# Masks taken off the matrix engine: block mask by GpSimd in batch rows 1 to 3, triangles of narrow score squares added in a shared bank by VectorE

## The reference

```python
xn = _layernorm(x, axis=-1)
x = x + _L0_attn_ref(xn, ...) + _L0_ffn_ref(xn, ...)

# attention: 16 heads of 16, 4 batches of 1024 tokens, width 256
q, k = (rope(q), rope(k))
att = jnp.einsum('bhqd,bhkd->bhqk', q, k) / scale
mask = jnp.tril(jnp.ones((t, t), dtype=bool))
att = jnp.where(mask, att, -jnp.inf)
att = jax.nn.softmax(att, axis=-1)
y = jnp.einsum('bhqk,bhkd->bhqd', att, v)

# feed-forward: 16 blocks of 64 hidden units, each token uses the 4 that its router ranks highest
prob = jax.nn.softmax(xf @ router_w.T + router_b, axis=-1)
_, idx = jax.lax.top_k(prob, TOPK)
mask = jnp.zeros((n, NBLK), bool).at[jnp.arange(n)[:, None], idx].set(True)
h = jnp.einsum('nd,ibd->nib', xf, w1b) + b1b
h = jax.nn.relu(jnp.where(mask[:, :, None], h, jnp.zeros((), h.dtype)))
y = jnp.einsum('nib,dib->nd', jnp.where(mask[:, :, None], h, 0.0), w2b) + b2
```

## Time and profile before

| | us |
|---|---|
| median of 3 runs | 829.46 (828.54 to 829.77) |
| profiled execution, its own time | 827.81 |
| its span, first to last instruction | 826.0 |
| TensorE busy in it | 812.7 (98%) |
| VectorE busy | 576.8 (70%) |
| ScalarE busy | 426.3 (52%) |
| GpSimd busy | 284.2 (34%) |

### The profile page before, as it was taken

The page is one execution under the profiler, slowest core; times in us unless marked ns, Lnnn a source line. Parts: engine busy times, 40 slices in busy tenths (PEclk is TensorE's granted clock), DMA queues, the critical chain, the costliest instruction groups (busy, mean ns, idle before and its releaser), DMA issues.

```text
span 826.0 us, 14866 instructions
## 1 busy us (share of the span) xinstructions
PE 812.7 (98%) x5275; PEld 490.6 (59%) x5275; DVE 576.8 (70%) x1785; ACT 426.3 (52%) x1018; POOL 284.2 (34%) x301
## 2 busy tenths in 40 slices
PE   7999999999999999999999999999999999999998
PEld 3677454544556655656666556664766556465764
DVE  6879787787998766675786866667676776767312
ACT  3523555564645645554564554645565454546552
POOL 4494249343650158067041028509400002000000
PEclk9999999999999999999999999999999999999999
DMA  8952515232514253240333215232070415000011
GB/s 266 275 163 78 168 54 166 93 90 92 166 61 136 80 143 142 65 122 19 100 121 76 93 53 166 91 91 92 3 216 2 116 54 142 15 15 16 15 58 52
DMA packets 53335, 81.91 MB, mean 99 GB/s; under 512 B 6796, under 2 KB 22092, under 8 KB 53260
## 3 DMA queue, kind: packets, MB, share of 16 engines
q1 hardware_dynamic: 53260, 80.95, 32.4%
HBM read 43.06 MB, written 37.88 MB: 98 GB/s over the span
## 4 chain that ended last, share of the span: by engine, by line
PE 92%; DVE 4%; ACT 2%; issue 1%; DMA 1%; SPq 0%; ACTq 0%; DVEq 0%
PE o_bank L1149 16%; PE banks L1074 15%; PE banks L1133 14%; PE banks L1049 14%; PE banks L1062 14%; PE banks L1023 7%; PE banks L1136 3%; PE banks L1032 3%; PE banks L1101 3%; PE banks L1053 2%; ACT probs L950 2%; DVE part_max L1342 1%; PE banks L1013 1%; DMA bqk_sb<-in_bk 1%; DVE o_norm L1379 1%
## 5 line engine op out<-in xcount | busy, mean ns | idle before, releaser
L950 ACT ACTIVATE probs<-banks 128x512 f32<-128x512 f32 (+3 forms) x768 | 328.0, 496 | 243.8 <-PE banks L1136 174.4
L1133 PE MATMUL banks<-q_st,k_st 99*128 99x512 bf16 (+3 forms) x768 | 234.8, 327 | 2.6 <-ACT probs L950 1.0
L1074 PE MATMUL banks<-k_st,q_st 96*128 96x512 bf16 (+3 forms) x768 | 228.7, 327 | 0.6 <-DVE part_max L1342 0.2
L1345 DVE CUSTOM_DVE_ANT_0 banks<-banks,tri,part_max 128x512 f32<-128x512 f32 (+3 forms) x256 | 128.9, 556 | 68.3 <-PE banks L1074 67.9
L1342 DVE TENSOR_REDUCE part_max<-banks 128x1 f32<-128x512 f32 x256 | 160.0, 677 | 17.6 <-PE banks L1074 17.2
L1345 DVE CUSTOM_DVE_ANT_0 banks<-banks,tri 128x512 f32<-128x512 f32 (+3 forms) x256 | 120.0, 515 | 34.4 <-PE banks L1074 33.5
L836 POOL TENSOR_SCALAR max_neg<-row_max 128x16 f32<-128x16 f32 x32 | 8.2, 255 | 382.1 <-DVE row_max L1345 382.1
L1049 PE MATMUL banks<-xnT,w_sb 128*128 128x256 f32 x512 | 134.5, 386 | 0.1
L1149 PE MATMUL o_bank<-probs,v_sb 128*17 128x512 f32 (+3 forms) x1536 | 133.2, 487 | 0.7 <-DVE o_norm L1379 0.7
L1062 PE MATMUL banks<-w_sb,hT 128*128 128x256 f32 x512 | 121.2, 382 | 0.0
L1074 PEld LDWEIGHTS banks<-k_st,q_st 96*128 96x128 bf16 x768 | 73.4, 98 | 73.6 <-issue 19.6
(11 more groups left out here) (100 smaller groups left out, 734.3 us busy)
## 6 DMA issues: line engine op xcount, KB each, us to landing
term_scratch<-pieces SPq DMA_DIRECT2D x84, 256.0 KB, 2.8
q_st<-term_scratch SPq DMA_DIRECT2D x16, 768.0 KB, 6.0
k_st<-term_scratch SPq DMA_DIRECT2D x16, 768.0 KB, 8.4
y_scratch<-o_norm SPq DMA_DIRECT2D x31, 256.0 KB, 2.1
acc<-in_x SPq DMA_DIRECT2D x8, 512.0 KB, 4.0
rope_sb<-y_scratch SPq DMA_DIRECT2D x15, 256.0 KB
out<-acc SPq DMA_DIRECT2D x7, 512.0 KB, 2.9
x_sb<-in_x SPq DMA_DIRECT2D x3, 1024.0 KB, 5.9
```

The source lines that it names most:

```text
L950: nc.scalar.activation(probs[:, h, PROBS_AT[u]:PROBS_AT[u] + w], filled("score", n, k, h)[:, 0:w], ACT.Exp, scale=SCALE).then_inc(s_out, 1)
L1074: nc.tensor.matmul(bank[:, 0:w], q_st[0:KROWS, at, h, i * P:(i + 1) * P], k_st[0:KROWS, at, h, c * HALF:c * HALF + w], start=True, stop=Tr ...
L1133: last = nc.tensor.matmul(bank[:, 0:w], k_st[0:SROWS, at, h, j * P:(j + 1) * P], q_st[0:SROWS, at, h, q0:q0 + w], start=True, stop=not dia ...
L1345: ins = nc.vector.tensor_tensor_reduce(bank[:, 0:w], bank[:, 0:w], tri[:, HALF - w:HALF], 1.0, least, ALU.add, ALU.max, to)
```

## The change

Two masks are made in another way.

The block mask. In batches 1 to 3 `hidden` has no mask matmul. The router's choice is kept as ones and zeros (`chosen`), turned by TensorE as before, written to DRAM by `store_chosen` and read back by `load_gates`, two transfers a quarter that spread each block's row over 64 partitions. GpSimd multiplies the relu's output by these gates, two hidden blocks of 256 tokens in one instruction (`gate`, 4 a quarter, 48 in all), and `ffn_tile` waits for GpSimd's count `gated` in place of ScalarE's. Batch 0 keeps the mask matmul; its `sel` is 16 partitions high and lies in one of the gate buffers.

The triangles. A unit of 256 or 128 columns is "narrow" (`masked_late`). Of a narrow unit 2 or 4 heads (`shared`) now write their squares side by side into one bank, without the mask matmul. VectorE adds the triangles of all of them in place in one instruction (`mask`), and ScalarE, which waits for VectorE's count `m_out`, takes one exponential of 512 columns. Each of the 16 groups has four narrow units, two of 256 and two of 128 columns: 16 mask matmuls of a group become 6 additions on VectorE (4 of 2x128 columns and 2 of 4x128), and 16 exponentials become 6. Over the program 256 mask matmuls become 64 and 32 additions, and 256 exponentials become 96. Units of 512 and 384 columns stay as they were.

The planner knows both (costs for a gate, a mask and a bank that is read later) and makes a new order. Small moves go with it: the last head group's `wo` is one transfer instead of four, late in the program, and two memsets go.

```diff
+def shared(k):
+
+    return HALF // width(k)
+
+
+def masked_late(n, k):
+
+    return diagonal(*UNITS[k]) and (width(k) <= QTR)
+
...
-        scored += 1
-        read(what, fill(what, width(k) + (P if diagonal(*UNITS[k]) else 0)), 11 * width(k) // 5 + 30)
+        scored += shared(k)
+        columns, late = shared(k) * width(k), masked_late(n, k)
+        at = fill(what, columns + (shared(k) * P if diagonal(*UNITS[k]) and not late else 0))
+        if late:
+            ready["vector"] = max(ready["vector"], clock + LATE) + 5 * shared(k) * P // 2 + 180
+            ready["scalar"] = max(ready["scalar"], ready["vector"] + HANDED - LATE)
+        read(what, at, 11 * columns // 5 + 30)
         exps[scored] = free[bank[what]]
...
+    def work_ready(what):
+        return what[0] != "ffn" or what[1] == 0 or gated.get((what[1], what[2] // 2, 2 * what[3] + 1), clock + 1) <= clock
...
+            def store_chosen(b):
+
+                if b >= 3:
+                    for buffer in range(2):
+                        sp.wait_ge(gates_in[buffer], (b - 2) * 2 * 32)
+                sp.wait_ge(m_out, M_COUNT["chosenT", b])
+                sp.dma_start(gate_scratch[b % 2], chosenT[:]).then_inc(chosen_out, 16)
+
+            def load_gates(b, q):
+
+                if b == 1 and q == 1:
+                    sp.wait_ge(s_out, S_COUNT["hid", 0, 3, FB - 1])
+                elif b > 1 or q > 1:
+                    sp.wait_ge(gated, (b * 4 + q - 5) * FB // 2)
+                if q == 0:
+                    sp.wait_ge(chosen_out, b * 16)
+                tokens = slice(q * QTR, (q + 1) * QTR)
+                for i in range(2):
+                    rows = gate_scratch[b % 2].rearrange("(m i) t -> i m t", i=2)[i, :, tokens]
+                    sp.dma_start(gates[i * 64:(i + 1) * 64, q % 2], rows.partition_broadcast(64)).then_inc(
+                        gates_in[q % 2], 16)
+
...
+            def gate(b, q, pair):
+
+                pool.wait_ge(s_out, S_COUNT["hid", b, q, 2 * pair + 1])
+                if pair == 0:
+                    pool.wait_ge(gates_in[q % 2], (b * 2 + q // 2 - 1) * 32)
+                blocks = slice(2 * pair, 2 * pair + 2)
+                nc.gpsimd.tensor_tensor(hT[:, blocks, :], hT[:, blocks, :], gates[:, q % 2, blocks, :],
+                                        ALU.mult).then_inc(gated, 1)
...
-                nc.scalar.activation(probs[:, h, PROBS_AT[u]:PROBS_AT[u] + w], filled("score", n, k, h)[:, 0:w],
-                                     ACT.Exp, scale=SCALE).then_inc(s_out, 1)
+                if masked_late(n, k):
+                    act.wait_ge(m_out, M_COUNT["score", n, k, h])
+                else:
+                    act.wait_ge(s_fill, S_FILLED["score", n, k, h])
+                bank = banks[:, BANK["score", n, k, h], :][:, 0:shared(k) * w].rearrange("p (h w) -> p h w", w=w)
+                nc.scalar.activation(probs[:, h:h + shared(k), PROBS_AT[u]:PROBS_AT[u] + w], bank, ACT.Exp,
+                                     scale=SCALE).then_inc(s_out, 1)
...
                 tokens = slice(q * QTR, (q + 1) * QTR)
                 for k in range(KB):
-                    nc.tensor.matmul(bank[:, 0:QTR], w1_sb[:, k, m * P:(m + 1) * P], xnT[:, b % 2, k, tokens],
-                                     start=(k == 0), stop=False)
-                if q == 0 and m == 0:
-                    pe.wait_ge(m_out, M_COUNT["unselT", b])
-                nc.tensor.matmul(bank[:, 0:QTR], sel[:, m, :], unselT[:, tokens], start=False,
-                                 stop=True).then_inc(s_fill, 1)
+                    last = nc.tensor.matmul(bank[:, 0:QTR], w1_sb[:, k, m * P:(m + 1) * P], xnT[:, b % 2, k, tokens],
+                                            start=(k == 0), stop=(b > 0 and k == KB - 1))
+                if b == 0:
+                    if q == 0 and m == 0:
+                        pe.wait_ge(m_out, M_COUNT["chosenT", 0])
+                    last = nc.tensor.matmul(bank[:, 0:QTR], sel[:, m, :], chosenT[:, tokens], start=False, stop=True)
+                last.then_inc(s_fill, 1)
 
             def ffn_tile(b, t, part):
 
                 bank = free_bank("ffn", b, t) if part == 0 else banks[:, BANK["ffn", b, t], :]
                 for m in range(part * FB // 2, (part + 1) * FB // 2):
-                    if t % 2 == 0:
+                    if t % 2 == 0 and b == 0:
                         pe.wait_ge(s_out, S_COUNT["hid", b, t // 2, m])
+                    elif t % 2 == 0 and m % 2 == 0:
+                        pe.wait_ge(gated, (b * 4 + t // 2 - 4) * FB // 2 + m // 2 + 1)
                     last = nc.tensor.matmul(bank[:, 0:D], hT[:, m, t % 2 * P:(t % 2 + 1) * P], w2_sb[:, m, :],
...
                     pe.wait_ge(max_rows[c], (n + 1) * 16)
                 bank = free_bank("score", n, k, h)
-                last = nc.tensor.matmul(bank[:, 0:w], k_st[0:SROWS, at, h, j * P:(j + 1) * P],
-                                        q_st[0:SROWS, at, h, q0:q0 + w], start=True, stop=not diagonal(c, j))
-                if diagonal(c, j):
-                    last = nc.tensor.matmul(bank[:, 0:P], tri_k, identb[:], start=False, stop=True)
-                last.then_inc(s_fill, 1)
+                bank = bank[:, 0:shared(k) * w].rearrange("p (h w) -> p h w", w=w)
+                mask = diagonal(c, j) and not masked_late(n, k)
+                for i in range(shared(k)):
+                    last = nc.tensor.matmul(bank[:, i], k_st[0:SROWS, at, h + i, j * P:(j + 1) * P],
+                                            q_st[0:SROWS, at, h + i, q0:q0 + w], start=(i == 0),
+                                            stop=i == shared(k) - 1 and not mask)
+                if mask:
+                    last = nc.tensor.matmul(bank[:, :, 0:P], tri_k, identb[:, None, :].broadcast_to([P, shared(k), P]),
+                                            start=False, stop=True)
+                last.then_inc(m_fill if masked_late(n, k) else s_fill, 1)
...
+            def mask(n, k, h):
+
+                w = width(k)
+                dve.wait_ge(m_fill, M_COUNT["score", n, k, h])
+                bank = banks[:, BANK["score", n, k, h], 0:shared(k) * w].rearrange("p (h w) -> p h w", w=w)[:, :, 0:P]
+                nc.vector.tensor_tensor(bank, bank, late_tri[:, None, :].broadcast_to([P, shared(k), P]),
+                                        ALU.add).then_inc(m_out, 1)
+
```

187 lines of the change are left out of this document (115 added, 72 removed).

## The result

The changed kernel takes **823.96 us** (823.91 to 824.19, four runs) where the kernel before took 829.00 beside it: a ratio of 0.9946, 95% interval [0.9935, 0.9958]. It is faster, as forecast and clear of the noise, but by 5.0 us and not by 19, and 824.0 lies above the range that ended at 821.

A forecast was written before the change was run, and what follows sets the result against it. The prediction took TensorE, issuing matmuls back to back (92% of the chain), as the bound. Terms: -24.1 TensorE, +4 and +2 VectorE, -2 ScalarE, +1 gates = -19.1, so 810 us, range 802.5 to 821.

The forecast's parts named there:

- A microsecond taken from TensorE is worth about a microsecond in batches 1 to 3: TensorE, masks removed: 13.6 us of triangles and 10.5 of block masks, 24.1 together, counted as gained in full.
- Batch 0's block mask costed at nothing: Batch 0's 32 remaining block mask matmuls got no term; only the 96 that go were counted, 10.5 us.
- In the start and the tail nothing large changes: Start and end of the program: no large change expected, and no term in the sum.
- VectorE's additions: Triangle additions, 48.8 us of VectorE: 4 us on the path in batch 0 and 2 us in the others.
- the term for batch 0: VectorE's additions in batch 0: a third of 12.2 us on the path, 4 us, bounds nothing and 12.2.
- Rival A: VectorE becomes the bound in batch 0: 12.2 us on the path, 3.7 in other batches, 820 us; chance 0.20.
- ScalarE's relief: Fewer exponentials: ScalarE 23 us less busy, 2 us credited in batch 0, bounds 0 and 5.8.
- The gates: GpSimd's gates between relu and `ffn_tile`, 51 to 57 us busy: 1 us of delay, between 0 and 11.
- Rival B: Everything hides: ScalarE's relief outweighs VectorE's additions, 24.1 and 2 us gained, 803 us; chance 0.09.
- Rival C: Runs ending in narrow units wait for score, addition, exponential: at 1.2 us each of 32, 849 us; chance 0.08.
- Rival D: Shared SBUF port: VectorE instructions with two SBUF operands wait out gates, 13 us on the path, 823 us; chance 0.03.

The follow-up runs named there:

- e11: The kernel before with the 256 narrow triangles and the 96 block masks left out and nothing in their place, order planned anew: 814.93 us.
- e7: e1 with each VectorE triangle addition cut to 2 of every 128 columns, same order and waits: 811.69 us.
- e9: e3 in the same order, with the gates, their loads and waits not executed, so no block mask in batches 1 to 3: 821.96 us.
- e15: The kernel before with the change's shared banks and merged exponentials, narrow triangles on no engine, block mask on TensorE (128 rows): 818.82 us.
- e10: The kernel before with the 256 narrow triangle matmuls left out and nothing in their place, order planned anew: 824.16 us.
- e1: The changed kernel with batch 0's block mask over 128 rows (zeros below row 16) instead of 16, same order: 816.90 us.
- e13: e5 with the planner's delay before the first gate raised from 20000 to 40000 columns: 824.27 us.
- e3: The kernel before with the change's GpSimd gates alone, batch 0's block mask over 128 rows, order planned anew: 823.89 us.
- e16: e10 in the same order, with each narrow exponential in batches 1 to 3 over one column in eight: 820.94 us.
- e2: The kernel before with its block mask over 16 rows in all 128 places: 852.80 us.
- e6: e1 with VectorE's triangle additions in batches 1 to 3 only; in batch 0 TensorE adds the triangles in shared banks: 817.62 us.
- e14: e1 with the planner's ScalarE costs raised towards the trace and the gates planned 40000 instead of 20000 columns after the choice's turn: 815.53 us.
- e5: e1 with TensorE adding the narrow triangles in the shared banks and no additions on VectorE: 833.43 us.

## Why the prediction was wrong, point by point

The runs add up, each term measured in its own pair of kernels: 828.0 (before) - 13.1 (both masks gone, e11) + 5.2 (additions, e7) + 1.9 (gates, e9) - 5.3 (shared banks, e15 over e10) = 816.7, and e1 has 816.9. With 7.1 for the 16 rows it is 823.8, and the change has 824.0. The pairs stand in different bases, and with e13 over e3 for the shared banks the sum would be 822.4 and 829.5, so the agreement to 0.2 us is luck. Firm are the 7.1 and the 5.2 us, each taken in the order of the change itself. The small moves (`wo`, the memsets) have no run of their own.

- **"A microsecond taken from TensorE is worth about a microsecond in batches 1 to 3": this step failed.** It was read from the chain's shares. 24.1 us came back as 13.1, and the narrow triangles of batches 1 to 3 as 0.6 of 10.2. The share says who was last on the way, not how far behind the next one is. Nor does the waits view of before say it: of its 18.0 us of scores waiting for exponentials batch 0 has 10.3 and batches 1 and 2 only 2.8, in 9 waits. With the narrow triangles gone (e10) it is 7.8 us there, in 25 waits: the readers were close behind, and the wait appeared when TensorE came sooner. e16 shows ScalarE's time in the narrow exponentials as a third of the missing part; the rest, VectorE's reads and the order among them, isn't settled.
- **Batch 0's block mask costed at nothing: this step failed too**, by 7.1 us, half of the miss of 14. (The other half comes from the 11.0 us that didn't come back, of which other terms made good a part.) "In the start and the tail nothing large changes" overlooked that the operand had 16 rows. The Trainium skill ("TensorEngine Tiling (Array Packing)", section "Key Properties") says that changing the tiling mode drains TensorE; it gives no price, and it doesn't say that a plain matmul of few rows is such a change. The traces agree with a cost at both edges (0.09 and 0.20 us in the opening, 0.10 and 0.10 in e2), but no run here separates a drain from another cost of the switch.
- **VectorE's additions**: 4 + 2 us forecast, 5.2 measured (e7, which leaves 17.6 of their 50.8 us in place); e6 fits the term for batch 0. Rival A, with 12.2 + 3.7, is refuted. This term was right.
- **ScalarE's relief**: -2 forecast; the runs have -5.3 in one pair (e15 over e10) and +0.4 in another (e13 over e3), so its size isn't settled. ScalarE lost 16.0 us (426.3 to 410.3) and not 23. The 0.3 us that the prediction takes from the Trainium skill ("ScalarE: Activation LUTs", section "Rules for kernel authors") is stated there for an activation whose bias is a pointer, one value for each partition. The trace agrees: at 256 columns the relu, which has such a bias, takes 475 ns and the exponential 388.
- **The gates**: +1 forecast, 1.9 measured (e9 under e3); `ffn_tile` waits for them 5 times, 3.6 us.
- **Rival B** (everything hides) is refuted by e7 and e11. **Rival C**: runs wait 13.2 us for exponentials, 11.2 before; refuted. **Rival D**: its mechanism is there, its size isn't. The mean of the Newton step's square went from 155 ns to 240, but that is eight squares as before and one of 907 ns, which starts while a gate runs and ends with it:

```profile
L1360 DVE TENSOR_TENSOR square<-rstd 128x8 f32<-128x8 f32 x9 | 2.2, 240 | 0.0
...
421.20 1.16 POOL L904 TENSOR_TENSOR hT<-hT,gates 128x512 f32<-128x512 f32 x1 [12.95 <-ACT hT L1029]
421.47 0.91 DVE L1360 TENSOR_TENSOR square<-rstd 128x8 f32<-128x8 f32 x1
```

So the rule that the prediction cites for this rival holds in the trace. Three more instructions meet a gate so: `logits<-raw_logits,rb_sb` takes 1.03 and 0.40 us for 0.28, and the copy `top<-top` 1.13 for 0.18. That is 2.6 us of VectorE in four places, for the 39 of the rival. The three additions of triangles that start during a gate take 0.43 to 0.69 us like the others. The prediction read the short squares of before as a sign that there is no such wait, but none of them overlaps an operation of GpSimd in that trace.

The forecast sum, corrected in its two failed terms (13.1 for 24.1, and +7.1), would have been 810 + 11.0 + 7.1 = 828; with 5.3 for 2 in the ScalarE term it would be 825.

## What to carry to other kernels

Before a share of the chain is turned into time, leave the work out and measure: one run without it prices the whole idea, and here it would have said 13, not 24 (what comes with the change, as the shared banks here, needs a price of its own). When a change shrinks an operand "on the way", read the new shape in the instruction (`16*128`) and price the edges to its neighbours, not its columns. An empty waits view isn't slack: it doesn't say how soon the next engine would be waited for. And look at the longest of a group, not at its mean alone (240 ns hid one of 907). Keep what a critical queue must do (here the split of the maxima) ahead of work that waits for a load, since one gate put ahead of it cost 9 us.

## What the runs showed of the hardware

A 256-column matmul over 16 rows between matmuls over 128 costs 0.19 us (e2, mean of 128) to 0.29 us (the opening) more than the same over 128 rows with zeros. Float32 matmuls over 64 rows by turns with 128-row ones start 0.31 to 0.32 us a record apart, for 0.216 among themselves. Scores over 99 and 96 rows beside 128-row ones show no such price; in e2's trace:

```profile
302.44 0.38 PE L1133 MATMUL banks<-q_st,k_st 99*128 99x512 bf16 x1
302.66 0.22 PE L1136 MATMUL banks<-identb,tri 128*128 128x128 bf16 x1
302.72 0.27 PE L1074 MATMUL banks<-k_st,q_st 96*128 96x256 bf16 x1
302.83 0.38 PE L1133 MATMUL banks<-q_st,k_st 99*128 99x512 bf16 x1
```

The loads of the gates, 256 KB each, in which 64 partitions get the same eight pieces of 256 elements, take more than twice as long to land as stores of that size (the last number, us), and as long as loads of `q_st` with three times the bytes. No run tells whether that is the many small pieces or the order in which they are asked for:

```profile
term_scratch<-pieces SPq DMA_DIRECT2D x84, 256.0 KB, 2.9
q_st<-term_scratch SPq DMA_DIRECT2D x16, 768.0 KB, 6.0
...
gates<-gate_scratch SPq DMA_DIRECT2D x24, 256.0 KB, 6.3
```

The one square of VectorE (two operands in SBUF) that starts while GpSimd multiplies by a gate ends with the gate, after 907 ns instead of 155; so it does in e1, e3 and e14 (906, 844 and 906 ns). Additions with one operand in a bank don't wait.

In e5 TensorE stood for 7.0 us; its last matmul record ends at 259.3 us, and the next starts at 266.1. Its granted clock is 1.00 up to 264.1 and 0.50, the level of 1.2 GHz, from 264.2 to 270.9; from 271 it is 1.00 again. The 4.8 us in which it works at half the clock cost 2.4 us more than the wait. The two together, 9.4 us, fit the 9.2 between e5 and e13.
